# The linear stage's first image is normalised inside the modulation stage's last rounds

## The reference

```python
x = x + _L0_conv_ref(_gn(x), ...)   # focal modulation: linear, three depthwise convolutions, gates
x = x + _L1_conv_ref(_gn(x), ...)   # layer norm, fp8 linear 64 -> 512, relu(a) * b, fp8 linear 256 -> 64
x = x + _L2_conv_ref(_gn(x), ...)   # gated scan with convolution kernels
x = x + _L3_conv_ref(_gn(x), ...)   # deformable 3x3 convolution

def _L1_conv_ref(x, ln_w, ln_b, w1, w2):
    mu = mean(x); var = mean(square(x - mu))            # over the 64 channels of each pixel
    h = (x - mu) * rsqrt(var + 1e-5) * ln_w + ln_b
    ab = _fp8_linear(h, w1)                             # rows scaled by max|h| / 448, rounded to fp8
    a, b = split(ab, 2)
    return _fp8_linear(relu(a) * b, w2)
```

## Time and profile before

| what | value |
|---|---|
| median of 3 runs | 5363.71 us |
| lowest and highest of them | 5361.05 and 5369.22 us |
| the profiled execution | 5375.03 us |
| its span | 5373.1 us, 93043 instructions |
| busy: PE, DVE, ACT, POOL | 3023.5, 3301.6, 1723.2 and 2852.9 us |
| shares of the span | 56%, 61%, 32% and 53% |

### The profile page before, as it was taken

How to read it: one execution, slowest core, us unless ns; L and a number is a source line. 1 busy time by engine, 2 the same in 40 slices (tenths; PEclk the granted TensorE clock), 3 DMA queues, 4 the chain that set the end, 5 groups by cost and what they waited for, 6 DMA issues and landing times. The chain is left out here.

```text
span 5373.1 us, 93043 instructions
## 1 busy us (share of the span) xinstructions
PE 3023.5 (56%) x39604; PEld 2643.3 (49%) x39604; DVE 3301.6 (61%) x4084; ACT 1723.2 (32%) x3209; POOL 2852.9 (53%) x2614
## 2 busy tenths in 40 slices
PE   2873235669644466569644466579744563554333
PEld 2872135559533355469533365469633453543222
DVE  4357843575678755675688666666779655454333
ACT  1223424721333235522234246422333242240000
POOL 1000000365566655665565666665666766777776
PEclk9965655569767666759666676769666755665555
DMA  6541174568633575658523566659433657554333
GB/s 165 121 83 23 29 137 129 151 141 190 137 92 106 123 195 165 177 131 194 135 80 108 148 169 183 163 138 208 126 98 97 164 165 179 174 164 124 103 105 93
DMA packets 776762, 727.31 MB, mean 135 GB/s; under 512 B 575244, under 2 KB 677036, under 8 KB 771916
## 3 DMA queue, kind: packets, MB, share of 16 engines
q1 hardware_dynamic: 651931, 381.46, 30.9%
q0 software_dynamic: 124416, 339.90, 21.9%
HBM read 601.34 MB, written 136.73 MB: 137 GB/s over the span
## 5 line engine op out<-in xcount | busy, mean ns | idle before, releaser
L2146 POOL DMA_INDIRECT e_gb<-corner_table,e_idx x2592 | 2838.3, 1095 | 2500.8 <-DMA e_cws<-cw_all 1043.8
L2208 DVE TENSOR_TENSOR e_vw<-e_gb,e_pc 128x1024 f32<-128x1024 f32 x576 | 773.0, 1369 | 692.7 <-DMA e_gb<-corner_table,e_idx 671.8
L2174 PE MATMUL e_pv<-shifts,e_vw 128*128 128x128 f32 x2768 | 557.5, 373 | 390.8 <-DVE e_vw L2215 390.8
L2174 PEld LDWEIGHTS e_pv<-shifts,e_vw 128*128 128x128 f32 x2768 | 461.1, 195 | 424.6 <-DVE e_vw L2215 401.8
L488 PE MATMUL e_pw<-wk,e_vt 128*64 128x64 f32 (+1 forms) x2880 | 333.7, 290 | 447.2 <-DVE e_xr L2226 236.6
L488 PEld LDWEIGHTS e_pw<-wk,e_vt 128*64 128x64 f32 (+1 forms) x2880 | 287.1, 197 | 512.0 <-issue 269.8
L2184 ACT ACTIVATE e_vt<-e_pv 128x512 f32<-128x512 f32 x288 | 182.4, 633 | 791.8 <-PE e_pw L2174 783.3
L502 PE MATMUL b_p<-b_x,b_tt 100*100 100x96 f32 x4096 | 375.6, 251 | 2.0 <-ACT b_x L815 2.0
L502 PEld LDWEIGHTS b_p<-b_x,b_tt 100*100 100x100 f32 x4096 | 370.3, 169 | 2.4 <-issue 1.6
L489 PE MATMUL e_pw<-wk,e_vt 128*64 128x64 f32 (+1 forms) x2880 | 335.0, 291 | 0.0
L2215 DVE TENSOR_TENSOR e_vw<-e_vw 128x1152 f32<-128x1152 f32 x230 | 322.5, 1402 | 7.9
(11 more groups left out here) (310 smaller groups left out, 7125.6 us busy)
## 6 DMA issues: line engine op xcount, KB each, us to landing
e_gb<-corner_table,e_idx POOLq DMA_INDIRECT x2592
d_px<-x_halo SPq DMA_DIRECT2D x32, 1152.0 KB
corner_table<-f_xn SPq DMA_DIRECT2D x128, 288.0 KB
b_tt<-zl_copies SPq DMA_DIRECT2D x128, 273.0 KB
b_tt<-zl_copies SPq DMA_DIRECT2D x128, 195.0 KB
f_xall<-xpad SPq DMA_DIRECT2D x10, 2400.0 KB
x_halo<-d_xo SPq DMA_DIRECT2D x128, 144.0 KB
d_wd<-wd_rows SPq DMA_DIRECT2D x8, 1890.0 KB
```

The source lines that it names most:

```text
L2146: nc.gpsimd.indirect_dma_start(self.gb[k][:, 4 * q:4 * q + 4, :].rearrange("p a c -> p (a c)"), None, T.table[m], off)\
L2174: last = nc.tensor.matmul(dst, vw[:, a, 2 * q:2 * q + nq, :].rearrange("p k c -> p (k c)"), T.ident[:, :], start=(a == 0), stop=(a == n - ...
L2208: v.tensor_tensor(dst, self.gb[k][:, 4 * k0:4 * k1, :].rearrange("p (k a) c -> p k a c", a=4), bc(w, [128, k1 - k0, 4, C], 3), ALU.mult).t ...
```

## The change

Four things change. `normalise(0)`, `rstd_h(0)` and `h_scaled(0)` of stage L move into stage C on DVE, and `square_h(0)`, `std_h(0)` and `layer_norm(0)` with them on ACT. Only `h_quantised(0)`, the transposes and their copies stay in the head of stage L. SP loads the input image 0 one round earlier. The buffers are laid out anew, with two unused gaps, so that `l_xn`, `l_ex` and `l_xs` lie behind everything of stage C and the small statistics lie in a hole of it. And the costs in `STEPS` follow: 16 more in C, 16 fewer in L.

```diff
 class StageC:
-    STEPS = [2, 8, 8, 4] + [8, 9, 12, 8] * (NI - 1) + [8, 1, 7, 6] + [6, 2, 1, 1]
+    STEPS = [2, 8, 8, 4] + [8, 9, 12, 8] * (NI - 1) + [8, 9, 7, 6] + [8, 2, 7, 1]
     # sp
+        if k == 3:
+            self.after.load(sp, G, 0)
         if k == 4:
-            self.after.load(sp, G, 0)
             self.after.load(sp, G, 1)
     # act, at the end of a step
+        if k == NI and p == 1:
+            self.after.square_h(act, G, 0)
+        if k == NI and p == 2:
+            self.after.std_h(act, G, 0)
+        if k == NI + 1 and p == 0:
+            self.after.layer_norm(act, G, 0)
     # dve, at the end of a step
+        if k == NI and p == 1:
+            self.after.normalise(dve, link, G, 0)
+        if k == NI and p == 3:
+            self.after.rstd_h(dve, link, G, 0)
+        if k == NI + 1 and p == 2:
+            self.after.h_scaled(dve, link, G, 0)
 class StageL:
-    STEPS = [14, 16] + [14, 7, 10, 10, 10, 9, 8] * (NI - 1) + [14, 8, 6, 10, 10, 8, 12] + [1]
+    STEPS = [6, 8] + [14, 7, 10, 10, 10, 9, 8] * (NI - 1) + [14, 8, 6, 10, 10, 8, 12] + [1]
-        self.xn = sb("xn", [128, J, C])
-        self.ex = sb("ex", [128, J, C])
         self.hq = sb("hq", [128, J, 2, C], BF16)
         self.ht = sb("ht", [128, J, 128], BF16)
+        self.ot = sb("ot", [128, J, C])
         self.ra = sb("ra", [128, 3, F])
+        sb("gap1", [128, 88])
+        self.s1, self.s2, ... self.so
         self.g = sb("g", [128, J, F])
...
+        sb("gap2", [128, 144])
+        self.xn = sb("xn", [128, J, C])
+        self.ex = sb("ex", [128, J, C])
         self.xs = sb("xs", [128, 3, J, C])
     # act
         if k == 0:
             self.st.enter(act, G, 3)
             between()
-            square_h(0)
-            std_h(0)
         if k == 1:
-            layer_norm(0)
             h_out(0)
             between()
     # dve
         if k == 0:
             self.st.enter(dve, G, 3)
-            normalise(0)
-        if k == 1:
-            rstd_h(0)
-            h_scaled(0)
             h_quantised(0)
```

More of the change, by code:

```diff
@@ L1084, in __init__ @@
         S = self.S
-        self.xn = sb("xn", [128, J, C])
-        self.ex = sb("ex", [128, J, C])
         self.hq = sb("hq", [128, J, 2, C], BF16)
         self.ht = sb("ht", [128, J, 128], BF16)
+        self.ot = sb("ot", [128, J, C])
         self.ra = sb("ra", [128, 3, F])
+        sb("gap1", [128, 88])
+        self.s1, self.s2, self.rs, self.bs, self.sx2, self.am, self.fs, self.hm = \
+            [sb(n, [128, J]) for n in ("s1", "s2", "rs", "bs", "sx2", "am", "fs", "hm")]
+        self.so = sb("so", [128, 2, J])
         self.g = sb("g", [128, J, F])
@@ L1201, in pe, with square_h, std_h, layer_norm @@
             self.st.leave(pe)
+    def square_h(self, act, G, m):
+        nc, S = self.nc, self.S
+        act.wait_ge(S.l_xn, NI * G + m + 1)
+        nc.scalar.activation(self.ex[:, :, :], self.xn[:, :, :], ACT.Square).then_inc(S.l_sqh, 1)
+    def std_h(self, act, G, m):
+        nc, S = self.nc, self.S
+        act.wait_ge(S.l_var, NI * G + m + 1)
+        nc.scalar.activation(self.rs[:, :], self.s2[:, :], ACT.Sqrt).then_inc(S.l_std, 1)
+    def layer_norm(self, act, G, m):
+        nc, S = self.nc, self.S
+        act.wait_ge(S.l_rstd, NI * G + m + 1)
+        for j in range(J):
+            last = nc.scalar.activation(self.xn[:, j, :], self.xn[:, j, :], ACT.Identity, scale=self.rs[:, j:j + 1], bias=self.bs[:, j:j + 1])
+        last.then_inc(S.l_ln, 1)
@@ new lines, in normalise @@
+    def normalise(self, dve, link, G, m):
+        nc, T, S, gn, v = self.nc, self.T, self.S, self.gn, self.nc.vector
+        xn, shape = self.xn[:, :, :], [128, J, C]
+        self.loaded(dve, G, m)
+        link(v.tensor_tensor(xn, self.xs[:, m % 3, :, :], gn.rows(T.norm1[:, m, 0, :], 128, J), ALU.mult))
+        v.tensor_tensor(xn, xn, gn.rows(T.norm1[:, m, 1, :], 128, J), ALU.add).then_inc(S.l_xn, 1)
+        dve.wait_ge(S.l_xn, NI * G + m + 1)
+        link(v.tensor_reduce(self.s1[:, :], xn, AX.X, ALU.add))
+        link(v.tensor_scalar(self.s1[:, :], self.s1[:, :], -1.0 / C, None, ALU.mult))
+        link(v.tensor_tensor(self.hm[:, :], self.s1[:, :], self.s1[:, :], ALU.mult))
+        dve.wait_ge(S.l_sqh, NI * G + m + 1)
+        link(v.tensor_reduce(self.s2[:, :], self.ex[:, :, :], AX.X, ALU.add))
+        link(v.scalar_tensor_tensor(self.s2[:, :], self.s2[:, :], 1.0 / C, self.hm[:, :], ALU.mult, ALU.subtract))
+        v.tensor_scalar(self.s2[:, :], self.s2[:, :], 0.0, 1e-5, ALU.max, ALU.add).then_inc(S.l_var, 1)
@@ new lines, in rstd_h, with h_scaled @@
+    def rstd_h(self, dve, link, G, m):
+        nc, T, S, gn, v = self.nc, self.T, self.S, self.gn, self.nc.vector
+        xn, shape = self.xn[:, :, :], [128, J, C]
+        dve.wait_ge(S.l_std, NI * G + m + 1)
+        polished(nc, link, self.rs[:, :], self.hm[:, :], self.s2[:, :])
+        v.tensor_tensor(self.bs[:, :], self.s1[:, :], self.rs[:, :], ALU.mult).then_inc(S.l_rstd, 1)
+    def h_scaled(self, dve, link, G, m):
+        nc, T, S, gn, v = self.nc, self.T, self.S, self.gn, self.nc.vector
+        xn, shape = self.xn[:, :, :], [128, J, C]
+        dve.wait_ge(S.l_ln, NI * G + m + 1)
+        link(v.tensor_tensor(xn, xn, bc(T.lnw[:, :], shape, 1), ALU.mult))
+        link(v.tensor_tensor(xn, xn, bc(T.lnb[:, :], shape, 1), ALU.add))
+        link(v.tensor_reduce(self.hm[:, :], xn, AX.X, ALU.max, apply_absolute_value=True))
+        link(v.tensor_scalar(self.hm[:, :], self.hm[:, :], 1e-12, 1.0 / FP8_MAX, ALU.max, ALU.mult))
+        link(v.reciprocal(self.s2[:, :], self.hm[:, :]))
+        link(v.tensor_tensor(xn, xn, bc(self.s2[:, :], shape, 2), ALU.mult))
@@ L1205, in act @@
         NT = J // 6 + J // 3
[L1207 to L1219, removed]
         def h_out(m):
@@ L1268, in act @@
             if ahead:
-                square_h(m + 1)
+                self.square_h(act, G, m + 1)
             g_scaled(m, 1)
@@ L1272, in act @@
             if ahead:
-                std_h(m + 1)
+                self.std_h(act, G, m + 1)
         if p == 3 and ahead:
-            layer_norm(m + 1)
+            self.layer_norm(act, G, m + 1)
         if p == 4:
@@ L1305, in quantise @@
             last.then_inc(done, 1) if done is not None else link(last)
[L1307 to L1332, removed]
         def h_quantised(m):
@@ L1387, in dve @@
         if p == 2 and ahead:
-            normalise(m + 1)
+            self.normalise(dve, link, G, m + 1)
         if p == 3:
@@ L1391, in dve @@
             if ahead:
-                rstd_h(m + 1)
+                self.rstd_h(dve, link, G, m + 1)
         if p == 4:
@@ L1397, in dve @@
             if ahead:
-                h_scaled(m + 1)
+                self.h_scaled(dve, link, G, m + 1)
         if p == 6:
```

## The result

The changed kernel takes 5348.26 us in the median of 20 runs (5328.64 to 5367.25), the kernel before on the same chips 5364.09 us (20 runs, 5356.71 to 5379.55). The ratio is 0.9965 with an interval of [0.9956, 0.9974]: by this ratio 18.8 us less, between 14 and 24 (the two medians by themselves lie 15.8 us apart). Forecast were 20.4 us. In the profiled executions the span went from 5373.1 to 5351.1 us.

The account below looks back on a forecast made before the run. The prediction took the end as bound by POOL's last run, started by one chain of stages; 2.8 + 3.6 + 3.6 + 10.4 = 20.4 us off the median 5363.7 gave 5343.3 us, range 5328 to 5363.

Parts of the forecast that it names:

- The chain: All stages: whatever shortens the chain in any group brings POOL's last run forward by as much; start about 20 us earlier.
- Group 0: Seam of C and L without tiles: layer_norm runs beside dve_scale and two hand-overs overlap; gain 2.8 us.
- Groups 1 and 2: Seams with three tiles re-placed in each: 0.8 us to h_quantised plus 2.8 us on PE; 3.6 us a group.
- The term for the transposes: PE in groups 1 and 2: tile 33's transposes in short form, taken as 2.2 us where it was 3.5.
- Group 3: Last group's seam: h_quantised 4.3 us earlier, wide product 6.1 us sooner behind it; gain 10.4 us.
- The things at nothing: SP's earlier load of image 0 and the new layout: no cost, with up to 5 us allowed either way.
- Behind the root: Rival, ACT: time needed between square root and layer_norm is exposed, 4.7 us or at most twice that; 5348 to 5353; chance 0.04.
- Only half arrives: Rival: gains on PE are lost to ACT's copies or tile work, only 8.7 us stay; 5355 us; chance 0.12.
- Swallowed: Rival: a transfer or POOL sets the pace between L and F, the seam is off the chain; 5364 us; chance 0.10.
- More: Rival: tile work on PE also hides in groups 1 and 2, hand-overs give 5 us; 5333 us; chance 0.10.
- Slower: Rival: one more tile's gathers fall into stage D's weight load, some 15 us in three groups; 5388 us; chance 0.07.

Follow-up runs that it names:

- e6: The changed kernel with work moved and new tile costs in group 3 only, groups 0 to 2 in the old order: 5356.31 us, ratio 0.9984.
- e4: The changed kernel plus eight idle DVE instructions, 6.4 us together, before DVE leaves stage C in every group: 5374.32 us, ratio 1.0012 to the kernel before.
- e5: The changed kernel itself, run again: 5343.09 us, ratio 0.9959 to the kernel before.
- e3: The kernel before with only the change's new layout of stage L's buffers: 5368.98 us, ratio 1.0001.
- e2: The changed kernel with the old cost lists, so the work moved but all tiles in their old places: 5339.69 us, ratio 0.9942 to the kernel before.
- e7: The changed kernel with old cost lists and tile places in groups 0 to 2, new in group 3: 5337.33 us, ratio 0.9945 to the kernel before.

## Why the prediction was right

- **The chain.** The step on which everything hung was that the seams of all four groups set the start of POOL's last run, and that run the end. That holds: e6 has group 3 alone at 9 us and the change at 19 to 22, and e4's delay arrives. The run from its first gather to its last keeps its length to 3.6 us in ten of the eleven traces of other kernels than the one before. Forecast was a start 20 us earlier; in the first trace it was 28, of which the seams are 25 and the rest is drift between them.
- **Group 0.** Forecast 2.8 us, measured 3.0 at `h_quantised`. `layer_norm` was to start 19.3 us behind the first moved instruction and did after 19.1; the wait of 4.6 us was called, and it is 4.63.
- **Groups 1 and 2.** `h_quantised` was forecast 49.1 us behind the start of `normalise` and ended after 49.05. The wide product was to follow by 6.1 us and did by 5.75. Forecast 3.6 us each; 3.9 and 3.8 at the `l_am` of the first image in the first trace (3.3 and 3.9 in e5). Behind that, two more us come by the end of stage L in group 2 and in one of two traces of group 1. I had not looked past the first image, and that is the one term mis-sized: 7.2 us forecast, 9.7 to 12.0 measured. The two us need neither the moved work nor the new places: e3, with neither work nor tiles moved, gains 2.1 and 1.5 us between the first image and the last in groups 1 and 2, e2 and e7 with the old places 1.2 to 1.5, and e6 nothing. For image 1 of group 1 the rows of transposes above put them down to where the TensorE clock rises; how much of them it makes in all was not added up. The term for the transposes has the same weakness: its two rows, 1.97 us for eight and 3.12 for sixteen, were taken at a granted clock of 0.50 and 0.62, and at 0.50 sixteen take 3.68. The 1.71 us of the eight in the changed kernel were at 0.62.
- **Group 3.** Forecast 40.7 us from the first moved instruction to the end of `h_quantised`, measured 40.5. L1343 (now L1364) 5.0 us behind it, measured 4.6. Together 10.4 forecast and 11.0 measured at the first image, 10.4 at the last.
- **The things at nothing.** The load was in time: L1239 waits for nothing. The layout is worth nothing that the times show (e3). Behind the root `layer_norm` lost nothing: the root starts at 448.38 and `layer_norm` at 448.52, with no idle time, and in the other three groups it is the same 0.14 us. By the Trainium skill (ScalarE: Activation LUTs, Table sets: the hidden batching unit) identity is among the functions in every set; the trace agrees.
- **The rivals.** *Only half arrives* (5355): the gains on PE are there in the traces, 6.5 us in group 3. *Swallowed*: e4 and e6. *More*, with the tile's work hidden in groups 1 and 2, did not happen, but e2 and e7 show a like sum of 28 to 32 us, in another way: the tile's work hidden on DVE beside `layer_norm`. *Slower*: the times exclude a loss of that size; whether a later gather falls into the load of stage D's weights was not looked for, and this mechanism was not tried by itself.
- **What was missed.** In groups 1 and 2 the prediction added tile 32's new place into the sum and got it right, but took the places as given. It did not ask whether another place would be better. The change gives away 4 us in each of these groups, as e2 and e7 show.
- **What stays open.** Between the seams the traces shift against each other by up to some 20 us over the whole span. The execution of before that was profiled lies 11 us above its median. How much of such drifts the clock makes was not measured.

## What to carry to other kernels

Where one chain of stages sets the end, ask of a moved step not whether it leaves the seam but which wait it lands in: here the same work gained 3 us in group 0 with `normalise` in place of a product, and 13 one round earlier: `normalise` then lay in a wait of 5.4 us for PE, and the wait of 4.6 us for `layer_norm` was gone too. When a long step of another engine gets onto the seam, leave a filler beside it: a tile of 4 us beside `layer_norm` was worth the 4 us that its new place lost. And where single executions spread by 20 us, compare the same stretch of two aligned traces; up to `h_quantised` the two traces of the changed kernel repeated to 0.15 us, by the end of stage L only to 2.3.

## What was not expected of the hardware

The spread of one program's times on one core: 5328.64 to 5367.25 us in 20 runs of the changed kernel, 0.7%, while the stretches at a seam of two executions agree to some 0.1 us (from the first moved instruction to `h_quantised` in group 3: -4.45 and -4.49 us against before). What varies lies behind and between them. One part is seen inside stage L: the same sixteen transposes take 1.97 to 3.68 us with the granted TensorE clock. And the time of a whole run goes with its mean granted clock. Of the 20 runs of the changed kernel the fastest (5328.64 us) has 0.685 and the slowest (5367.25) 0.673; of the 25 runs of the kernel before beside e5 the fastest (5341.61) has 0.687 and the slowest (5390.98) 0.672. That the clock makes the difference in time is not shown by this: both could follow from something else, such as the length of the waits between.
